# 16-head attention on one core: shift rows sent by one transfer from ScalarE's queue, maxima negated ahead of the next selects, later weights loaded behind the first stack

## What is computed

```python
x = x + _L0_attn_a_ref(_layernorm(x), Wq_w, Wq_b, Wk_w, ...)   # causal
x = x + _L0_ffn_ref(...)
x = x + _L0_attn_b_ref(_layernorm(x), Wq, bq, Wk, ...)         # rope, all keys
x = x + _L0_ffn_ref(...)  # then five more layers: L1 attention, mlp, fp4 ...
# in both attentions:
dot  = jnp.einsum('bhqd,bhkd->bhqk', q, k)       # causal: -inf above the diagonal
attn = jax.nn.softmax(dot * scale, axis=-1)
out  = jnp.einsum('bhqk,bhkd->bhqd', attn, v) @ Wo.T + bo
```

## Time and profile before

| | |
|---|---|
| three runs | 2376.65, 2382.59, 2406.39 us |
| the profiled execution | 2384.68 us, its span 2382.7 us |
| PE busy / DVE / ACT / POOL | 1830.9 / 1492.7 / 967.3 / 697.8 us |
| mean granted TensorE clock | 0.88 of full |
| first attention (`aa`) | from the start to about 575 us |
| second attention (`ab`) | from about 632 to about 1190 us |

### The profile page before, as it was taken

How to read it: one execution, slowest core, us unless ns; L and a number is a source line. 1 busy time by engine, 2 the same in 40 slices (tenths; PEclk the granted TensorE clock), 3 DMA queues, 4 the chain that set the end, 5 groups by cost and what they waited for, 6 DMA issues and landing times. The chain is left out here.

```text
span 2382.7 us, 37722 instructions
## 1 busy us (share of the span) xinstructions
PE 1830.9 (77%) x12781; PEld 982.9 (41%) x12781; DVE 1492.7 (63%) x4005; ACT 967.3 (41%) x1598; POOL 697.8 (29%) x788
## 2 busy tenths in 40 slices
PE   2777777676569898988857999999997756678566
PEld 0233333232312322322234666666665534445344
DVE  3545555454657776766555666666655489755997
ACT  0344444344326555655635444444443321233221
POOL 4333334322542222211030000000001466600665
PEclk9878878787659999999979999999999978789787
DMA  6222222220022223233000000000000000000000
GB/s 173 55 50 49 46 54 50 41 42 1 9 64 57 49 46 50 55 55 54 2 1 1 2 2 2 2 2 2 2 2 1 1 1 0 1 1 0 5 13 18
DMA packets 71735, 62.99 MB, mean 26 GB/s; under 512 B 11785, under 2 KB 69385, under 8 KB 71561
## 3 DMA queue, kind: packets, MB, share of 16 engines
q1 hardware_dynamic: 71560, 60.74, 13.2%
HBM read 45.38 MB, written 15.20 MB: 25 GB/s over the span
## 5 line engine op out<-in xcount | busy, mean ns | idle before, releaser
L600 DVE TENSOR_REDUCE ab_M<-ps 128x1 f32<-128x512 f32 x512 | 334.8, 687 | 147.1 <-PE ps L473 145.3
L595 DVE CUSTOM_DVE_ANT_0 aa_masked<-ps,aa_mask_row 128x384 bf16<-128x384 f32 (+3 forms) x512 | 228.6, 487 | 234.4 <-PE ps L473 233.2
L410 ACT ACTIVATE ab_probs<-ps 128x1024 f32<-128x1024 f32 x256 | 261.6, 1024 | 175.4 <-PE ps L495 174.5
L410 ACT ACTIVATE aa_probs<-ps 128x1024 f32<-128x1024 f32 (+1 forms) x192 | 169.1, 881 | 205.1 <-PE ps L495 204.4
L473 PE MATMUL ps<-ab_KS,ab_QS 96*128 96x512 bf16 x512 | 206.1, 408 | 42.8 <-DMA ab_KS<-ab_parts_dram 23.6
L1548 PE MATMUL ps<-gate_up,fp_xT 128*128 128x352 f32 x256 | 129.7, 673 | 90.7 <-DVE fp_xh L1590 89.3
L473 PE MATMUL ps<-aa_KS,aa_QS 96*128 96x384 bf16 (+3 forms) x512 | 143.3, 342 | 49.0 <-DMA aa_KS<-aa_parts_dram 35.1
L321 POOL TENSOR_SCALAR_AFFINE_SELECT aa_probs<-aa_probs 128x256 f32<-128x256 f32 (+1 forms) x192 | 92.9, 484 | 300.0 <-ACT aa_probs L410 299.9
L495 PE MATMUL ps<-ab_QS,ab_KS 128*128 128x512 bf16 x512 | 158.0, 392 | 22.7 <-DMA ab_QS<-ab_nm_dram 22.7
L473 PEld LDWEIGHTS ps<-ab_KS,ab_QS 96*128 96x128 bf16 x512 | 50.3, 98 | 236.9 <-DVE ab_M L600 170.4
L651 POOL TENSOR_TENSOR la_rstd<-la_vare,mhalf 128x4 f32<-128x4 f32 x16 | 16.1, 1007 | 442.8 <-DVE la_vare L646 442.8
(11 more groups left out here) (310 smaller groups left out, 3899.1 us busy)
## 6 DMA issues: line engine op xcount, KB each, us to landing
aa_QS<-aa_parts_dram SPq DMA_DIRECT2D x144, 64.0 KB
aa_KS<-aa_parts_dram SPq DMA_DIRECT2D x144, 64.0 KB
ab_QS<-ab_parts_dram SPq DMA_DIRECT2D x144, 64.0 KB
ab_KS<-ab_parts_dram SPq DMA_DIRECT2D x144, 64.0 KB
aa_parts_dram<-aa_splitq SPq DMA_DIRECT2D x24, 128.0 KB, 1.8
aa_parts_dram<-aa_splitk SPq DMA_DIRECT2D x24, 128.0 KB, 1.8
ab_parts_dram<-ab_splitq SPq DMA_DIRECT2D x24, 128.0 KB, 1.8
ab_parts_dram<-ab_splitk SPq DMA_DIRECT2D x24, 128.0 KB, 1.9
```

What stands on the lines that cost most here:

```text
L410: act.activation(v(probs[u % 4][:]), v(src), ACT.Exp, scale=scale).then_inc(scores_free, 1)
L595: last = v.tensor_tensor_reduce(masked[U % 4][:, o * stride:o * stride + width], src[:, o, :], mask_row[:, 512 - width:512], 1.0, 4 * NEG, ...
L600: v.tensor_reduce(M[gq % 2][:, heads[0]:heads[-1] + 1, qt], src, AX.X, ALU.max).then_inc(max_free, 1)
```

## The change

1. **Negation earlier.** `negate` has its own time, 1.02 slots after the start of its quad instead of 1.30; the turning on PE and the copy on ACT stand at 1.19 instead of 1.30.
2. **Shift rows by one transfer.** `send_nm` moves from SP to ACT, at 1.29: one transfer from `nmT` straight to `QS`, no DRAM, no wait for a landing between.
3. **Item work earlier.** stat, spread, norm, turn, xT, split, store and the first half of the stack stand about 0.3 slots earlier, q 0.32, k 0.26, the second half 0.25.
4. **Zero rows by transfers.** The memsets of `QS` and `KS` are replaced, at the start of each attention, by six transfers from a tile of zeros (56 rows of `QS`, 24 and 30 rows of `KS`, for both buffers) and two of the signs. They move 3.6 MB per attention. PE waits for them before the first slot of items 0 and 1.
5. **Loads.** The 30 transfers of later weights are issued behind the first item's 36 stack transfers. DVE starts its statistics when x of item 0 has landed, not the weights too; the small memsets of `V` and of one PSUM bank move behind the normalization.

```diff
-    at(-4, "bias", 0, 0)
+    at(-3.85, "bias", 0, 0)
...
-            at(t0 + 0.02 + 0.09 * t, "stat", n, 0, t)
-        at(t0 + 0.39, "spread", n, 0)
+            at(t0 - 0.28 + 0.09 * t, "stat", n, 0, t)
+        at(t0 + 0.09, "spread", n, 0)
...
-        at(t0 + 1.38, "q", n, 0)
-        at(t0 + 1.58, "k", n, 0)
+        at(t0 + 1.06, "q", n, 0)
+        at(t0 + 1.32, "k", n, 0)
...
-                at(t0 + 1.46 + 0.44 * a + 0.11 * i, "split", n, a, i)
-        at(t0 + 2.38, "store", n, 0)
-        at(t0 + 2.50, "half", n, 0, 0)
+                at(t0 + 1.17 + 0.44 * a + 0.11 * i, "split", n, a, i)
+        at(t0 + 2.10, "store", n, 0)
+        at(t0 + 2.20, "half", n, 0, 0)
...
-            at(g + 1.30, "nm", n, q)
+            at(g + 1.02, "negate", n, q)
+            at(g + 1.19, "nm", n, q)
+            at(g + 1.29, "send", n, q)
...
     def sync(sp):
+        none = over(core["zeros"][:].bitcast(BF16), 1, HEADS // 2)
+        blank = lambda tile, lo, hi: tile[lo:hi].rearrange("p (a b) t -> p a (b t)", b=2)
+        for i in range(2):
+            sp.dma_start(blank(QS[i], ROWS, P), none[ROWS:P]).then_inc(pad_loaded[i], 16)
+            sp.dma_start(blank(KS[i], ROWS, SHIFT_AT), none[ROWS:SHIFT_AT]).then_inc(pad_loaded[i], 16)
+            sp.dma_start(blank(KS[i], SHIFT_AT + SHIFT_ROWS, P), none[SHIFT_AT + SHIFT_ROWS:P])\
+                .then_inc(pad_loaded[i], 16)
+            sp.dma_start(KS[i][SHIFT_AT:SHIFT_AT + SHIFT_ROWS], over(core["signs16"][:], 1, HEADS))\
+                .then_inc(pad_loaded[i], 16)
...
-            sp.wait_ge(misc_free, uses_of_misc("nm", n, q))
-            sp.dma_start(nm_dram[q], nmT[q][:]).then_inc(nm_stored, 16)
-            sp.wait_ge(nm_stored, 16 * (gq + 1))
-            sp.dma_start(QS[n % 2][SHIFT_AT:SHIFT_AT + SHIFT_ROWS, 4 * q:4 * q + 4],
-                         nm_dram[q].rearrange("(r j t) k -> r j (t k)", r=SHIFT_ROWS, j=4)).then_inc(nm_loaded[q], 16)
-
-        walk({"store": store, "half": stack, "nm": send_nm})
+            if n == 0 and half == 1 and causal:
+                core["load_rest"](sp)
+
+        walk({"store": store, "half": stack})
...
+            act.wait_ge(misc_free, uses_of_misc("nm", n, q))
+            act.dma_start(QS[n % 2][SHIFT_AT:SHIFT_AT + SHIFT_ROWS, 4 * q:4 * q + 4]
+                          .rearrange("r j (t k) -> r (j t) k", t=4),
+                          nmT[q][:]).then_inc(nm_loaded[q], 16)
...
-                pe.wait_ge(stack_loaded[q // 2], 16 * STACK_DMAS * (n + 1) + (0 if q else 16 * min(n + 1, 2)))
+                pe.wait_ge(stack_loaded[q // 2], 16 * STACK_DMAS * (n + 1))
+                if n < 2:
+                    pe.wait_ge(pad_loaded[n], 16 * 4)
```

More of the change, by code:

```diff
@@ L203, in attention @@
     misc4 = misc.rearrange("p (t c) -> p t c", t=4)
-    set_up, bv_spread, pad_cleared = sem("set_up"), sem("bv_spread"), sem("pad_cleared")
+    set_up, bv_spread = sem("set_up"), sem("bv_spread")
+    pad_loaded = [sem(f"pad_loaded{i}") for i in range(2)]
     stats_ready, vare_ready, rstd_ready = sem("stats_ready"), sem("vare_ready"), sem("rstd_ready")
@@ L322, in clear_future @@
                             pattern=[[0, len(heads)], [1, P]], channel_multiplier=-1).then_inc(probs_masked, 1)
-        does = {"spread": root, "turn": turn, "split": split_part, "clear": clear, "nm": negate}
+        does = {"spread": root, "turn": turn, "split": split_part, "negate": negate}
         if causal:
@@ L345, in stack @@
                 sp.wait_ge(scores_ready, N2 * (QUADS * (n - 2) + 2 * (half + 1)))
-            elif half == 0:
-                sp.wait_ge(pad_cleared, n + 1)
-                sp.dma_start(KS[n][SHIFT_AT:SHIFT_AT + SHIFT_ROWS], over(core["signs16"][:], 1, HEADS))\
-                    .then_inc(stack_loaded[0], 16)
             h = slice(HEADS // 2 * half, HEADS // 2 * (half + 1))
@@ L537, in vector @@
     def vector(v):
-        for i in range(2):
-            v.memset(V[i][:, :, :, DH:DH + 1], 1.0)
-        v.memset(ps[:, SUMS, :], 0.0)
-        v.drain().then_inc(set_up, 1)
-        if causal:
-            v.wait_ge(set_up, 2)
         def total_bias(n, q, gq, i):
             v.wait_ge(misc_full, uses_of_misc("bias", 0))
+            core["await_first"](v)
             v.tensor_tensor(bias[:], misc[:, 0:P], w["bo"][:], ALU.add).then_inc(misc_free, 1)
@@ L551, in stat @@
             if n == 1 and t == 0:
-                v.wait_ge(core["loaded"], 16 * core["loads"])
+                v.wait_ge(core["x_loaded"], 16)
             v.bn_stats(stats[:, t, :], X[:, 4 * n + t, :]).then_inc(stats_ready, 1)
@@ L571, in norm, with prepare @@
                             ALU.subtract, ALU.mult).then_inc(xn_ready, 1)
-        def clear(n, q, gq, i):
+        def prepare(n, q, gq, i):
             if n == 0 and i == 0:
-                for t in (QS[0], KS[0]):
-                    v.memset(t[64:P], 0.0)
-                v.drain().then_inc(pad_cleared, 1)
+                for i in range(2):
+                    v.memset(V[i][:, :, :, DH:DH + 1], 1.0)
+                v.memset(ps[:, SUMS, :], 0.0)
+                v.drain().then_inc(set_up, 1)
+                if causal:
+                    v.wait_ge(set_up, 2)
         def split_part(n, a, gq, i):
@@ L1636, in build @@
         first_loaded = whole.enter_context(nc.semaphore("first_loaded"))
+        first_x = whole.enter_context(nc.semaphore("first_x"))
+        core["x_loaded"] = x_loaded = whole.enter_context(nc.semaphore("x_loaded"))
         core["loaded"] = loaded = whole.enter_context(nc.semaphore("loaded"))
@@ L1658, in build @@
                 early = len(loads)
-        core["loads"] = len(loads) - early + 1
+        core["loads"] = len(loads) - early
         programs = []
@@ L1664, in build @@
                 programs.append(kind(core, items, own, **how["args"]))
+        core["await_first"] = lambda eng: eng.wait_ge(first_loaded, 16 * early)
         block = whole.enter_context(nc.Block())
@@ L1684, in sequences, with load_rest @@
                 return tensor[lo:hi].rearrange("b (t p) c -> p (b t) c", p=P)
-            sp.dma_start(core["X"][:, 0:4], sequences(dram["x"], 0, 1)).then_inc(first_loaded, 16)
+            def load_rest(sp):
+                for t, src in loads[early:]:
+                    sp.dma_start(t[:], src).then_inc(loaded, 16)
+            core["load_rest"] = load_rest
+            sp.dma_start(core["X"][:, 0:4], sequences(dram["x"], 0, 1)).then_inc(first_x, 16)
             for t, src in loads[:early]:
                 sp.dma_start(t[:], src).then_inc(first_loaded, 16)
-            sp.dma_start(core["X"][:, 4:], sequences(dram["x"], 1, items)).then_inc(loaded, 16)
-            for t, src in loads[early:]:
-                sp.dma_start(t[:], src).then_inc(loaded, 16)
+            sp.dma_start(core["X"][:, 4:], sequences(dram["x"], 1, items)).then_inc(x_loaded, 16)
+            if layers[0] is not ATTN_A:
+                load_rest(sp)
             sp.wait_ge(consts, 3)
@@ L1743, in _ @@
         def _(v):
-            v.wait_ge(first_loaded, 16 * (early + 1))
+            v.wait_ge(first_x, 16)
+            if layers[0][0] is not attention:
+                v.wait_ge(first_loaded, 16 * early)
             v.wait_ge(consts, 3)
```

33 lines of the change are left out of this document (15 added, 18 removed).

## The result

Four runs of the changed kernel have a median of 2260.4 us (2250.2 to 2264.6), against 2393.9 (2376.7 to 2406.4) for four of the kernel before: a ratio of 0.944, 95% interval 0.936 to 0.952. The forecast was 2262 us. The profiled execution has a span of 2262.8 us and a mean granted clock of 0.904 (before 2382.7 and 0.88).

What follows compares the result with a forecast made beforehand. PE was taken to bound both attentions, with 127 and 50 us idle. Terms of -91 (first attention), -27 (second) and -3 (start) made -121 us, to a median of 2262 us, range 2215 to 2325.

Steps and rivals of the forecast that it cites:

- The turning, -57: First attention, PE's wait to turn the negated maxima: of 76.2 us 19 stay, once per item behind the splits; -57 us.
- Shift rows, -20: First attention, PE's wait for the shift rows' transfer: of 22.5 us 2 stay, the small transfer overtaking the stack; -20 us.
- rival 3: Shift rows late anyway: ACT's transfer waits behind the stack, half of 64 sends 3 us late; 2342 us, chance 0.07.
- Stack, +4: First attention, PE's wait for the stack: as late as before, 1.0 to 2 us per item, 8.1 becoming 12; +4 us.
- cross-check of 12.9: First attention's slot length in us, from 15.8 before, by taking the summed -91 us over 31 slots.
- Bank `misc`, +6: First attention, PSUM bank `misc`: q closely followed by the turning, k by the tail, two waiting places per item; +6 us.
- rival 1: New small waits between engines in the first attention take the old ones' place, no clock gain; 2313 us, chance 0.22.
- Clock, first attention, -24: First attention, PE's granted clock of 0.81: fewer long waits give back part of a 28 to 67 us loss; -24 us.
- Second attention, -27: Second attention: waits for shift rows and stack go but for 4 us, -23, and clock gives -4; -27 us.
- Start, -3 and 0: First scores of the two attentions: at 47 us in the first, -3 us; pads in time in the second, 0.
- rival 5: Pads slow: +11 and +8 us at the two starts instead of -3 and 0; 2284 us, chance 0.06.
- rival 4: ACT is held by its issues of the sends, stopping exponentials and PE behind them; 2518 us, chance 0.03.

Runs made afterwards that it cites:

- e2: Kernel before, with only the shift rows sent by one direct transfer on ACT's queue: 2336.5 us, ratio 0.979.
- e11: Changed kernel, with the shift rows sent through DRAM on SP's queue again: 2439.7 us, ratio 1.016.
- e1: Kernel before, with only the negation and its turning earlier (1.02 and 1.19 slots): 2350.3 us, ratio 0.987.
- e6: Kernel before, with early negation and the direct send on ACT's queue together, nothing else: 2295.5 us, ratio 0.963.
- e4: Changed kernel, with the rows of signs sent again ahead of each half of each stack: 2235.4 us, ratio 0.938.
- e9: Changed kernel, with the stack's second half held until the third quad's shift rows of the item before have landed: 2265.4 us, ratio 0.948.
- e10: Changed kernel with zero rows by memsets and signs ahead of each half stack (2211.3 us), plus the second half held for the shift rows: 2220.1 us, ratio 0.929.
- e5: Changed kernel, with 16 KB of zeros over 128 partitions sent to a spare tile ahead of each half stack: 2267.4 us, ratio 0.953.

## Why the prediction was right in sum and wrong in its terms

**The turning, -57.** Right: 76.2 fell to 17.2, that is -59, or -63 over the same slots. The reason was right too: once per item the negation stands behind the splits (2.3 us in the usual case, where 2.7 was reckoned).

**Shift rows, -20.** Wrong: -3.5. The step that failed is "from another queue, and one hop instead of two, I take 2 to 5 us". With SP's queue empty the last packet moves 1.5 us after the issue. But one send per item is issued during the stack, and PE had its shift rows 12.5 us after the issue. The send itself makes this load: while it was SP's, the wait for its landing kept the two halves of the stack apart (154.9 to 166.9 us in the kernel before), and without it they go out back to back, after (18 transfers from 146.93 right behind 18 from 140.68) as in e2, which has the old times (148.16 behind 141.89). I had not listed this consequence of the edit. The lower bound that I gave ("0 if the transfer queues behind the stack as before") is what happened in the first attention; rival 3 had the mechanism, for one send in four instead of two. The Trainium skill, "DMA: Bandwidth & Descriptors", section "Queues, rings and completion order", says that an engine turns between the queues that have work, at packet boundaries. The trace agrees with it once the send has begun: its 34 packets lie between some 170 of the stack. That the send would therefore overtake the stack was my conclusion, and the trace refutes it: some 730 stack packets went first.

Yet the direct send is the edit that the rest rests on. e11 shows that without it the kernel takes 2440 us. I priced it by the wait that it takes away, 20 us, not by the wait that the other edits would make without it. I also priced its issue at SP's 0.32 us, and it took 0.62 on ACT; e2 shows no cost of it.

**Stack, +4.** About 0 in all, 8.1 to 8.2 us, but by two errors that cancel. The steady items' wait nearly went, to 2.0 us: I had counted the four slots until the stack is needed at 11 us each, against my own cross-check of 12.9, and with 12.7 as measured the 36 us behind q end before the fourth slot does (49.5 against 50.9 us). And the weights behind the first stack, to which I gave no price since they are "needed only at the next layer", held the second item's stores back: 6.2 us.

**Bank `misc`, +6.** About 0: 5.2 to 4.5 us. The places of q and k in the order made no wait. What came instead was not in the sum: 17.6 us more for ACT's copy `aa_C`, 0.7 us a time, 26 times. It is rival 1's kind (a new small wait), with a handover that I had not looked at; e1 ties it to the negation.

**Clock, first attention, -24.** Too small. PE's busy time per slot was 353/480 x 15.8 = 11.6 us and is 305.5/380 x 12.7 = 10.2; over 31 slots that is 43 us for the same products, and the stretches at the lower level say the same, 75 us lost before and 32 after. -50 was the end that I had given. The step that failed is the bound, "28 to 67": it supposed that the idle time lies in those stretches, at least as much as elsewhere. PE worked 151 of their 196 us, 77%, where it worked 74% of the whole window; so 75 us were lost to the low clock, more than the upper bound. Over the same slots the waits add up to -63 (turning) - 3.5 - 0.6 + 17.6 - 4.3 (selects) - 0.2 (maxima) + 4.3 (issue) = -50, with the clock -93, against -96 measured. So the first attention's sum was right by luck: the clock gave 19 us more than reckoned where the shift rows gave 17 less, and the 17.6 us of `aa_C` stood against 11 us of stack and `misc` that never came and 6 more of the turning.

**Second attention, -27.** Too small by 22 us. The waits for transfers went as said, 26.9 to 1.0, and `ab_C` took 9 back. What was mis-sized is the clock: at 0.95 I took 4 of the 22 us that it could give, and it went to 0.98. Its stretches at the lower level, before and after:

```profile
sum 63.20, PE 54.32 PEld 13.58 DVE 35.16 ACT 14.95 POOL 17.87; mean PE 7.76 PEld 1.94 DVE 5.02 ACT 2.14 POOL 2.55
...
sum 23.40, PE 20.41 PEld 6.09 DVE 17.82 ACT 3.04 POOL 10.50; mean PE 6.80 PEld 2.03 DVE 5.94 ACT 1.01 POOL 3.50
```

Half of 54 less half of 20 is 17 us given back. Before, there was one stretch from the start to 703.5 us and six more, and each of the six began during a PE wait of 1.6 us or more for a transfer, or within 1.3 us of its end (one such wait, of 2.0 us, had none). With these waits gone, one is left but for the start and the end. Waits and clock make some -38 of the -49; the rest isn't in the views. e6 against the changed kernel puts 33 us of the second attention on the remaining edits, of which only the earlier item work touches its slots.

**Start, -3 and 0.** Wrong: +12.0 and +9.1, near rival 5's +11 and +8, to which I had given 6 in 100. Two steps failed. Pads were put at 250 GB/s "nearer to the loads since pads have long rows"; they ran at 141 to 158, near the 136 that the stack's rows had given. The stack went out at 43.2 us, 6 later than before and 9 later than reckoned. The other 6 us were in no case of mine: the stack itself ran at 69 instead of 115 GB/s, since the signs no longer went out right ahead of it (e4 puts them back, and has 4 of the 6). I had read the 17.1 us of a steady stack and the 12.9 of the first one in the rows, and had not asked why they differ.

**The range and the rivals.** The chances gave the forecast 0.48; what came is 145 us less in the two attentions, where 118 were forecast, and 21 more at the starts plus 4 in the rest, where -3 was forecast. That this ends 2 us from the forecast is luck: terms of 17 to 24 us missed on both sides. And the four runs of the kernel before have a median of 2393.9 us, not the 2382.6 that the forecast started from; by these medians the gain is 133 us, not 121. ACT was not held by its issues: rival 4 is excluded by e2, where all 64 sends are on ACT and the second attention is 29 us shorter.

## What to carry to other kernels

Price an edit that takes a transfer off a busy queue by what the other edits will ask of that queue, not by today's wait: the same send was worth 57 us alone and 179 us in company (50 and 172 by ratios). Where a small transfer has a deadline, look at what is in flight on any queue when it is issued; a queue of its own did not let it pass here, and making the bulk transfer faster (e4) paid where holding it back (e9, e10) did not. And when two instances of one transfer take different times in the trace, as the first stack and the later ones did here, find the reason before moving anything that stands next to them.

## What the hardware did that I had not expected

- **Behind a narrow transfer the stack ran faster.** Stack transfers go to 8 partitions each and keep the DMA engines at a share of 0.57. Behind the signs, a transfer into 2 partitions, they ran at 115 GB/s (before) and 90 to 107 (e4, 44 to 54 us); without it, or behind one over 128 partitions, at 69 to 72 (after) and 75 to 77 (e5), at shares of 0.57 to 0.59. The Trainium skill, "DMA: Bandwidth & Descriptors", section "Why a DMA increments its semaphore by 16 and not by 1", states that a transfer is spread over as many engines as the largest number up to 16 that divides its slowest dimensions: 8 for the stack, 2 for the signs. The share of 0.57 is near 8 of 16, and of the 72 packets of a stack transfer 64 carry 1 KB and 8 are small. My reading, argued and not shown, is that the signs put two of the eight engines out of step with the others, so that they no longer ask for the same memory at the same moment. The later stacks of the changed kernel vary from 78 to 113 packets per us with no transfer ahead, and what sets them apart stayed open.
- **Zero rows copied within the chip's SBUF** ran at 141 to 158 GB/s with all engines busy (share 0.92 to 0.98), where loads from DRAM had 298 GB/s at 1.04.
- **A small transfer on ACT's queue waited for some three quarters of what SP's queue had in flight**, 705 to 811 packets in six items, and its issue took 0.62 us, against 0.32 on SP.
